# A graph attention layer: rows without neighbours in two batches, and the dense loop ahead of the last list

## The chip, the cores and the metric

One core of a Trainium2 chip. The metric is the device time of one launch in microseconds. The engines are PE (TensorE), DVE (VectorE), ACT (ScalarE), POOL (GpSimd) and SP (SyncE); each runs its own list of instructions in order and waits on semaphores.

## The reference

`x` is 8192 x 128, `adj` 8192 x 8192 int32 with about 4 ones in a row, `attn` 256 x 1.

```python
h = jnp.maximum(_layernorm(x, axis=-1), 0.0)
s_i = h @ attn[:128]
s_j = h @ attn[128:]
e = jax.nn.leaky_relu(s_i + s_j.T, negative_slope=0.2)
e = e + jnp.where(adj > 0, 0.0, -1.0e9)
out = x + jax.nn.softmax(e, axis=1) @ h
```

A row with neighbours is the softmax over those few. A row without any is a softmax over all 8192 columns, each lowered by 1e9.

## The kernel before

The 256 MB of `adj` are read once. Row `64 p + t` lies in partition `p` of tile `t`; 64 tiles make 32 pairs. `h_all`, `x_all` (64 tiles each) stay in SBUF, and `h` with its scores is also written to a table in HBM, from which rows are gathered.

For each pair `p`:

- SP loads four half tiles of 128 x 4096 int32 into the four slots of `adj_ring`. Each load waits until ACT has taken the sign of the half tile before it in its slot (`signed`).
- ACT turns a half tile into signs (bf16, L533) and counts the neighbours (`degree`). It waits for PE to have packed the half tile three before.
- PE packs the signs of eight column chunks into `words` by matmuls (`pack_tile`, L1160).
- DVE takes the largest words (`max_tile`, L656), finds the neighbours' numbers (`find_pair`, ends with `near_id`, L701), and flags rows with too many neighbours for the 12 slots of a pair (`flag_pair`). PE ranks the flagged rows (`rank_pair`, L1171), DVE gives them keys (`key_pair`), PE copies them into a list (`list_pair`).
- POOL gathers 12 neighbours for each row (`gather_pair`, L455: one indirect DMA a slot).
- Two steps later DVE scores pair `g = p - 2` (`score_pair`), ACT takes the exponential, DVE mixes (`add_pair`: 16 multiply-adds of 128 x 128, L797), SP stores the pair.

The flagged rows of eight pairs make one list of at most 128 rows with 16 slots, four lists in all (`m` 0 to 3): `find_deep` at the first step after the eight pairs, POOL's `gather_m` in parts in the steps behind it (DEEP_PARTS), `score_deep` and `add_deep` in step DEEP_MIX = 7 of the next eight, `store_m` by POOL. The last list has no next eight: its gathers and its mixing stand behind the stream. `add_deep` of list 2 stands there too, at step 31.

Rows without neighbours whose scores are extreme ("lone" rows; for all others the table's row of means serves) are handled once, behind the last pair, for at most 128 rows: `lone_mark` (which rows), `lone_compact` (one-hot matrices and ranks, PE helps, L1210 to L1213), `lone_bounds` (scores spread over the partitions by PE, L1220, L1223), then four `lone_part`s over 16 tiles of columns each: three DVE instructions of 128 x 2048 (L949, L954, L958), one exponential on ACT (L581), 16 (of 64) matmuls on PE (L1229). `lone_end` divides and adds `x`.

The dense loop ("far") is for rows that fit nowhere: it runs over `far_tiles` x `far_parts`, at least once each, and computes rows of one tile against 256 columns by the plain formula. With these inputs it runs once and stores nothing that counts. In DVE's order before: pairs 29, 30, 31 mixed, sizing of the loop (L1042 to L1069), last list (L847 to L884), `lone_end`, then the loop, which waits for POOL to have seen the last stores land (`far_free`).

Of the kernel before, what the change touches and what calls it, by code (L numbers as in the profile page):

```python
# [5 lines left out]
def graph_attention_kernel(nc: bass.Bass, x: bass.AP, adj: bass.AP, attn: bass.AP, out: bass.AP):  # L6
# [40 lines left out]
    DEEP_PARTS = (3, 3, 3, 3, 2, 2)  # L47
    DEEP_MIX = 7
# [13 lines left out]
    LC = 4  # L62
    LT = TILES // LC

# [9 lines left out]
    with ctx:  # L74
# [124 lines left out]
        lonely = end(TILES, fp32)  # L199
        lone_at, lone_top = end(TILES, fp32), end(8, fp32)  # L200
        lone_here = end(4, bf16)
        lone_key, lone_si = end(LONE, fp32), end(LONE, fp32)
        lone_eq, lone_pick = end(LONE * TILES, fp32), end(LONE * TILES, fp32)
        lone_hot = end(LONE * P, fp32).rearrange("p (k e) -> p k e", k=LONE)
        lone_few, lone_many, lone_spill = end(1, fp32), end(1, fp32), end(1, fp32)
        lost = end(TILES, fp32)
        lone_si_b, lone_max_raw, lone_max_leaky, lone_max = end(P, fp32), end(P, fp32), end(P, fp32), end(P, fp32)
        lone_absent, lone_id, lone_inv = end(1, fp32), end(1, i32), end(1, fp32)
        lone_x, lone_out = end(D, fp32), end(D, fp32)
        far_h = end(DB * COLS, fp32).rearrange("p (k c) -> p k c", k=DB)  # L210
        assert taken[0] <= HALF
        lone_p = adj_ring[:, 2:4, :].rearrange("p h w -> p (h w)").bitcast(fp32)
# [19 lines left out]
        lone_rank = words[1][:, BANK:BANK + LONE]  # L232
        lone_rec = words[1][:, BANK + 16:BANK + 17]
        lone_spread = words[0][:, BANK:BANK + P]
        lone_sum = words[2][:, BANK:BANK + ONE + 1]
# [52 lines left out]
        lone = sem("lone")  # L288
        lone_here_ready = sem("lone_here_ready")
        lone_ranked = sem("lone_ranked")  # L290
        lone_hot_ready = sem("lone_hot_ready")
        lone_spread_out = sem("lone_spread_out")
        lone_id_ready = sem("lone_id_ready")
        lone_x_in = sem("lone_x_in")
        lone_masking = sem("lone_masking")
        lone_masked = sem("lone_masked")
        lone_exp = sem("lone_exp")
        lone_summed = sem("lone_summed")
        lone_out_ready = sem("lone_out_ready")
        lone_stored = sem("lone_stored")  # L300
# [6 lines left out]
        far_h_in = sem("far_h_in")  # L307
        far_used = sem("far_used")
# [25 lines left out]
        LONE_MARK = 4  # L334
        LONE_HOT = 8
        LONE_IDS = 5
# [8 lines left out]
        def _(sp):  # L345
# [23 lines left out]
            for g in range(PAIRS - 4, PAIRS):  # L369
                store_pair(g)  # L370
# [4 lines left out]
            with sp.Fori(0, tiles) as t:  # L375
                with sp.Fori(0, parts) as c:
# [5 lines left out]
                        .then_inc(far_adj_in, 16)  # L382

        @block.gpsimd
        def _(pool):
# [63 lines left out]

            def gather_pair(p):  # L450
# [32 lines left out]

            for p in range(PAIRS):
# [9 lines left out]
            pool.indirect_dma_start(  # L494
                out=lone_x, out_offset=None, in_=x,
                in_offset=bass.IndirectOffsetOnAxis(ap=lone_id[:, 0:1], axis=0),
                bounds_check=last_row, oob_is_err=False).then_inc(lone_x_in, 16)
# [3 lines left out]
            pool.indirect_dma_start(  # L501
                out=out, out_offset=bass.IndirectOffsetOnAxis(ap=lone_id[:, 0:1], axis=0),
                in_=lone_out, in_offset=None,
# [782 lines left out]
```

## Time and profile before

| | |
|---|---|
| median of 3 runs | 868.03 us (866.7 to 868.43) |
| the profiled execution | 867.93 us |
| its span, first to last instruction | 866.2 us |
| busy share: DVE, POOL, ACT, PE | 66%, 66%, 60%, 53% |
| moved by DMA | 301.56 MB |

Times in the rows below are microseconds from the span's start. "L656" is a line of the kernel. A row of the timeline has start, duration, engine, line, operation, what it writes and reads, how many in a row, and in brackets how long its engine was idle before it and what ended that.

### The profile page before, as it was taken

How to read it: one execution, taken by the hardware profiler on the slowest of the kernel's cores; microseconds unless marked ns; L12 is line 12 of the kernel's file. 1: busy time of each engine (PE TensorE's matmuls, PEld its weight loads, DVE VectorE, ACT ScalarE, POOL GpSimd, SP SyncE). 2: the span in 40 equal slices, each digit the busy share in tenths (PEclk: the TensorE clock that was granted, in tenths of full speed). 3: DMA queues.
4: the chain of work that ended last, by engine and by line, in shares of the span. 5: the costliest groups of instructions: out<-in, count | busy, mean ns of one | idle time of the engine just before them, and what ended most of it. 6: DMA issues, size and time to landing. Idle time of an engine off the chain costs nothing.

```text
span 866.2 us, 7055 instructions
## 1 busy us (share of the span) xinstructions
PE 460.1 (53%) x1605; PEld 191.2 (22%) x1633; DVE 569.3 (66%) x2273; ACT 521.1 (60%) x357; POOL 571.0 (66%) x527
## 2 busy tenths in 40 slices
PE   0665465655555665566555656556566455623601
PEld 0332122221212222122222222222222122213600
DVE  7998266565676666656766465568656566668981
ACT  1895676666676666676666666667666677600200
POOL 6631776666567777666678777667776867758810
PEclk9998777676886678776788686876767788665955
DMA  8799999999999999999999999999999999511000
GB/s 346 286 382 404 399 406 409 410 410 410 406 408 409 410 408 409 405 410 411 404 406 410 408 411 406 414 405 412 404 405 403 408 391 404 196 25 27 18 16 14
DMA packets 39515, 301.56 MB, mean 348 GB/s; under 512 B 10611, under 2 KB 16948, under 8 KB 22065
## 3 DMA queue, kind: packets, MB, share of 16 engines
q1 hardware_dynamic: 24176, 277.23, 79.1%
q0 software_dynamic: 15296, 23.88, 8.0%
q8 instruction: 13, 0.21, 0.1%
q14 instruction: 30, 0.24, 0.1%
HBM read 303.63 MB, written 8.91 MB: 361 GB/s over the span
## 4 chain that ended last, share of the span: by engine, by line
DMA 69%; issue 13%; DVE 11%; ACT 5%; PE 1%; DVEq 0%; POOL 0%; SPq 0%; ACTq 0%; POOLq 0%
DMA adj_ring<-in_adj_dram 68%; ACT sign_ring L533 3%; DVE mixed L797 1%; DVE one_hot L609 1%; ACT h_all L544 1%; DVE adj_ring L954 1%; DVE adj_ring L958 1%; DVE adj_ring L949 1%; DVE mixed_m L879 1%; DMA x_all<-in_x_dram 1%; PE words L1160 0%; DVE codes L616 0%; DVE codes L619 0%; PE words L1220 0%; PE words L1223 0%
## 5 line engine op out<-in xcount | busy, mean ns | idle before, releaser
L533 ACT ACTIVATE sign_ring<-adj_ring,half_neg 128x4096 bf16<-128x4096 int32 x128 | 474.6, 3708 | 226.4 <-DMA adj_ring<-in_adj_dram 226.4
L455 POOL DMA_INDIRECT near<-h_table,near_id x384 | 443.8, 1156 | 198.9 <-issue 109.2
L1160 PE MATMUL words<-sign_ring,pack_w 128*128 128x512 bf16 x1004 | 357.2, 516 | 282.3 <-ACT sign_ring L533 279.6
L656 DVE MAX8 cand<-words 128x8 f32<-128x256 f32 x256 | 91.1, 418 | 223.9 <-PE words L1160 223.8
L1160 PEld LDWEIGHTS words<-sign_ring,pack_w 128*128 128x128 bf16 x1024 | 114.1, 121 | 516.7 <-ACT sign_ring L533 357.2
L797 DVE SCALAR_TENSOR_TENSOR mixed<-near,weight_n,mixed 128x128 f32<-128x128 f32 x448 | 120.3, 345 | 0.0
L470 POOL DMA_INDIRECT near_m<-h_table,id_m x64 | 79.1, 1235 | 19.5 <-issue 19.5
L1152 PE MATMUL words<-place,place_w 128*128 128x512 bf16 x120 | 47.2, 478 | 1.1 <-issue 1.0
L1142 PE MATMUL listing<-h_all 128*1 128x128 f32 x128 | 20.4, 335 | 33.7 <-ACT h_all L544 33.7
L581 ACT ACTIVATE adj_ring<-adj_ring 128x2048 f32<-128x2048 f32 x4 | 7.6, 1910 | 49.8 <-DVE adj_ring L958 49.8
L1179 PEld LDWEIGHTS listing<-cand,one_hot 128*128 128x128 f32 x128 | 28.1, 271 | 12.6 <-issue 6.5
L1229 PE MATMUL words<-h_all,adj_ring 128*128 128x129 f32 x128 | 18.8, 316 | 15.7 <-ACT adj_ring L581 15.7
L1179 PE MATMUL listing<-cand,one_hot 128*128 128x34 f32 x128 | 23.3, 317 | 2.5 <-DVE one_hot L745 2.5
L533 ACT ACTIVATION_READ_ACCUMULATOR sign_ring<-adj_ring,half_neg 128x1 f32 x128 | 23.9, 186 | 0.0
L434 POOL TENSOR_SCALAR h_all<-x_all,codes 128x128 f32<-128x128 f32 x16 | 13.0, 825 | 14.5 <-DVE codes L628 14.5
L1142 PEld LDWEIGHTS listing<-h_all 128*1 128x1 f32 x128 | 12.8, 102 | 41.4 <-issue 27.1
L672 DVE TENSOR_TENSOR codes<-cand_i,code_mask 128x512 int32<-128x512 int32 x32 | 21.9, 684 | 0.0
L1229 PEld LDWEIGHTS words<-h_all,adj_ring 128*128 128x128 f32 x128 | 18.1, 229 | 16.4 <-ACT adj_ring L581 16.4
L642 DVE TENSOR_TENSOR near<-h_all,mixed 128x2048 f32<-128x2048 f32 x8 | 21.5, 2683 | 0.0
L797 DVE SCALAR_TENSOR_TENSOR mixed<-near,weight_n,x_all 128x128 f32<-128x128 f32 x64 | 19.8, 350 | 1.1
L544 ACT ACTIVATE h_all<-x_all,codes 128x128 f32<-128x128 f32 x48 | 18.8, 480 | 0.2 <-DVE codes L628 0.2
L647 DVE TENSOR_REDUCE h_all<-near 128x16 f32<-128x2048 f32 x8 | 18.3, 2288 | 0.3
(213 smaller groups left out, 431.4 us busy)
## 6 DMA issues: line engine op xcount, KB each, us to landing
adj_ring<-in_adj_dram SPq DMA_DIRECT2D x128, 2048.0 KB, 18.9
near<-h_table,near_id POOLq DMA_INDIRECT x384, 6.4
h_table<-h_all POOLq DMA_DIRECT2D x4, 1056.0 KB, 12.2
x_all<-in_x_dram SPq DMA_DIRECT2D x4, 1024.0 KB, 9.6
out_dram<-mixed SPq DMA_DIRECT2D x32, 128.0 KB, 18.5
near_m<-h_table,id_m POOLq DMA_INDIRECT x64, 6.2
adj_ring<-h_table SPq DMA_DIRECT2D x1, 132.0 KB, 3.1
mixed<-in_L_gnn_attn_dram SPq DMA_DIRECT2D x1, 128.0 KB, 6.5
```

The costliest lines, as they stand in the source:

```text
L455: pool.indirect_dma_start(out=near[:, p % RING, k, :], out_offset=None, in_=table, in_offset=bass.IndirectOffsetOnAxis(ap=near_id[:, p % I ...
L470: pool.indirect_dma_start(out=near_m[:, k, :], out_offset=None, in_=table, in_offset=bass.IndirectOffsetOnAxis(ap=id_m[:, k:k + 1], axis=0 ...
L533: nc.scalar.activation(sign_ring[:, n % 4, :], adj_ring[:, n % 4, :], ACT.Sign, bias=half_neg[:, :], accum_out=degree[:, t, h:h + 1]).then ...
L544: nc.scalar.activation(h_all[:, t, 0:D], x_all[:, t, :], ACT.Relu, bias=shift[:, t:t + 1], scale=rstd[:, t:t + 1]).then_inc(h_ready, 1)
L656: last = nc.vector.max(out=cand[:, p % 2, t % 2, 8 * q:8 * q + 8], in_=words[t % 3][:, q * PART:(q + 1) * PART])
L672: nc.vector.tensor_tensor(codes[:, :, :, :].rearrange("p a w c -> p (a w) c"), cand_i[:, :, :].rearrange("p a w -> p (a w)").unsqueeze(2). ...
L797: ins = nc.vector.scalar_tensor_tensor(acc, near[:, e, slot, 0:D], weight_n[:, a * own + k:a * own + k + 1], base, ALU.mult, ALU.add)
L1142: last = nc.tensor.matmul(listing[0:1, 0:D], h_all[:, t, ONE:ONE + 1], h_all[:, t, 0:D], start=(t == 0), stop=(t == TILES - 1))
L1152: nc.tensor.matmul(at[:, k * BANK:(k + 1) * BANK], place_w[:, :], place[:, k * BANK:(k + 1) * BANK], start=True, stop=False)
L1160: last = nc.tensor.matmul(at[:, k * BANK:(k + 1) * BANK], pack_w[:, c, :], sign_ring[:, n % 4, o + k * BANK:o + (k + 1) * BANK], start=Fal ...
L1179: last = nc.tensor.matmul(listing[:, 0:REC], one_hot[:, p % 2, a, :], cand[:, p % 2, a, :], start=(p % SEG == 0 and a == 0), stop=(p % SEG ...
L1229: last = nc.tensor.matmul(lone_sum, lone_p[:, t * P:(t + 1) * P], h_all[:, t, 0:ONE + 1], start=(t == 0), stop=(t == TILES - 1))
```

## The change

Two batches of lone rows: batch 0 holds those of pairs 0 to 22 (at most 64 rows, four parts of 16 tiles, one of three buffers each) and is worked off in the loop, steps 22 to 30; batch 1 those of pairs 23 to 31 (at most 32 rows, two parts of 32 tiles) behind the stream. A part has 1024 elements per partition in both. Batch 0's scratch lies in the first 40 tiles of `x_all`, which are no longer read then; so the dense loop loads its tile of `x` anew (`far_x`). The dense loop stands ahead of the last list's mixing on DVE, ACT and POOL; its sizing moves up between the compaction and the bounds of batch 1, and behind its parts. The lists' gathers are made in five parts instead of six, and their mixing in step 6 instead of 7. Pair 29 is scored before tile 62's maxima and mixed before tile 63's. The stores of pairs 30 and 31 are issued by ACT.

```diff
-    DEEP_PARTS = (3, 3, 3, 3, 2, 2)
-    DEEP_MIX = 7
+    DEEP_PARTS = (3, 3, 3, 3, 4)
+    DEEP_MIX = 6
-    LC = 4
-    LT = TILES // LC
+    EARLY = 23
+    FIRST_STEP = EARLY + 1
+    LAST = 1
+    LONE_CAP = (64, 32)
+    LONE_PARTS = (4, 2)
+    LONE_BUFS = 3
+    DEAD = 40
...
@@ gpsimd
+            pool.sem_inc(far_free, 1)
...
             for p in range(PAIRS):
                 gather_pair(p)
+                if p == FIRST_STEP + 2:
+                    load_lone(0)
...
             store_m(SEGS - 2)
-            pool.wait_ge(lone_id_ready, 1)
-            pool.indirect_dma_start(out=lone_x, ...)
+            store_lone(0)
+            load_lone(LAST)
             gather_m(SEGS - 1, range(0, DEEP))
-            store_m(SEGS - 1)
-            pool.wait_ge(lone_out_ready, 1)
-            pool.indirect_dma_start(out=out, ..., in_=lone_out, ...)
             pool.wait_ge(sizes_ready, 2)
...
-            pool.wait_ge(stored_m, 16 * SEGS)
-            pool.wait_ge(lone_stored, 16)
-            pool.sem_inc(far_free, 1)
+            for e in range(2):
+                pool.wait_ge(stored[e], 16 * PAIRS // 2)
             with pool.Fori(0, tiles) as t:
...
+            store_m(SEGS - 1)
+            store_lone(LAST)
+            pool.wait_ge(stored_m, 16 * SEGS)
+            pool.wait_ge(lone_stored[0], 16)
+            pool.wait_ge(lone_stored[LAST], 16)
@@ scalar
             def exp_step(p):
...
+                if FIRST_STEP <= p - 1 < FIRST_STEP + LONE_PARTS[0]:
+                    exp_lone(0, p - 1 - FIRST_STEP)
             for p in range(1, PAIRS):
                 sign_tile(2 * p, (0,))
                 exp_step(p - 1)
                 sign_tile(2 * p, (1,))
-                sign_tile(2 * p + 1)
-            exp_step(PAIRS - 1)
+                sign_tile(2 * p + 1, (0,))
+                if p == PAIRS - 1:
+                    exp_step(p)
+                sign_tile(2 * p + 1, (1,))
...
             exp_pair(PAIRS - 2)
+            store_pair(PAIRS - 2)
             exp_pair(PAIRS - 1)
-            exp_m(SEGS - 1)
+            store_pair(PAIRS - 1)
...
+            exp_m(SEGS - 1)
@@ vector
+            def lone_step(p):
+                if p == FIRST_STEP - 2:
+                    lone_mark(0)
+                if p == FIRST_STEP - 1:
+                    lone_compact(0)
+                if p == FIRST_STEP:
+                    lone_bounds(0)
+                if 0 <= p - FIRST_STEP < LONE_PARTS[0]:
+                    lone_part(0, p - FIRST_STEP)
+                if 0 <= p - FIRST_STEP - 3 < LONE_PARTS[0]:
+                    lone_add(p - FIRST_STEP - 3)
+                if p == FIRST_STEP + 3 + LONE_PARTS[0] - 1:
+                    lone_end(0)
...
-                max_tile(2 * p)
+                if p < PAIRS - 1:
+                    max_tile(2 * p)
                 for g in mixes:
                     score_pair(g)
+                if p == PAIRS - 1:
+                    max_tile(2 * p)
...
                 key_pair(p - 1)
+                if p == PAIRS - 1:
+                    for g in mixes:
+                        add_pair(g)
                 max_tile(2 * p + 1)
...
                 if p == PAIRS - 1:
-                    lone_mark()
+                    lone_mark(LAST)
                     key_pair(p)
+                    lone_compact(LAST)
                     find_deep(SEGS - 1)
-                    add_deep(SEGS - 2)
-                    lone_compact()
-                    lone_bounds()
-                    for c in range(LC):
-                        lone_part(c)
-                for g in mixes:
-                    add_pair(g)
-                if m >= 0 and p % SEG == DEEP_MIX and p < PAIRS - 1:
+                    mark_severe()
+                    lone_bounds(LAST)
+                    for c in range(LONE_PARTS[LAST]):
+                        lone_part(LAST, c)
+                    size_loop()
+                    dve.sem_inc(far_used, 1)
+                if p < PAIRS - 1:
+                    for g in mixes:
+                        add_pair(g)
+                if m >= 0 and p % SEG == DEEP_MIX:
                     add_deep(m)
+                lone_step(p)
...
-            score_deep(SEGS - 1)
-            add_deep(SEGS - 1)
-            lone_end()
             dve.wait_ge(sizes_ready, 2)
...
-            dve.wait_ge(pair_mixed, PAIRS)
...
+            score_deep(SEGS - 1)
+            add_deep(SEGS - 1)
+            lone_end(LAST)
@@ tensor, in rank_pair
+                if p >= FIRST_STEP - 1:
+                    pe.wait_ge(lone[0], LONE_MARK + LONE_HOT)
+                if p >= FIRST_STEP:
+                    pe.wait_ge(lone_id_ready[0], 1)
+                    pe.wait_ge(lone[0], LONE_MARK + LONE_HOT + LONE_IDS)
+                if 0 <= p - FIRST_STEP - 3 < LONE_PARTS[0]:
+                    pe.wait_ge(lone[0], LONE_MARK + LONE_HOT + LONE_IDS + p - FIRST_STEP - 2)
```

`mark_severe` and `size_loop` are the old sizing (L1042 to L1069) cut in two. `lone_add` adds a part's PSUM sum to an accumulator in SBUF. In PE's order, `lone_ranks(0)` stands at the end of step 23, `lone_spreads(0)` of step 24, the matmuls of batch 0's parts of steps 26 to 29.

## Rows read from the trace of the kernel before

**Rows 1.** The head of the page.

```profile
span 866.2 us, 7055 instructions
```

**Rows 2.** Engines' busy time in one pair's stretch (instructions), granted clock, DMA share, GB/s.

```profile
core 0: us, PE busy (x) PEld busy (x) DVE busy (x) ACT busy (x) POOL busy (x), PEclk, DMA share, GB/s
670.00:692.00 22.00, 11.11 (x37) 3.88 (x35) 13.53 (x60) 14.97 (x8) 17.59 (x15) 0.74 1.00 401
```

**Rows 3.** Timeline: a ranking on PE, DVE's next step, ACT's last sign.

```profile
612.53 0.17 PE L1171 MATMUL rank<-flag,before 128*128 128x2 bf16 x1
...
617.34 1.42 DVE L656 MAX8 cand<-words 128x8 f32<-128x256 f32 x4
...
755.26 3.71 ACT L533 ACTIVATE sign_ring<-adj_ring,half_neg 128x4096 bf16<-128x4096 int32 x1 [1.42 <-DMA adj_ring<-in_adj_dram]
```

**Rows 4.** Timeline of DVE: maxima of tiles 61, 62, 63.

```profile
740.02 1.43 DVE L656 MAX8 cand<-words 128x8 f32<-128x256 f32 x4 [7.54 <-PE words L1160]
...
752.43 1.42 DVE L656 MAX8 cand<-words 128x8 f32<-128x256 f32 x4 [1.44 <-PE words L1160]
...
762.71 1.43 DVE L656 MAX8 cand<-words 128x8 f32<-128x256 f32 x4 [5.60 <-PE words L1160]
```

**Rows 5.** Timeline of DVE behind the stream, up to the lone rows' end.

```profile
768.71 0.16 DVE L735 TENSOR_TENSOR prior<-prior,flag 128x1 bf16<-128x1 bf16 x1
...
771.80 0.19 DVE L810 CAST cand_m<-listing 128x32 int32<-128x32 f32 x1 [1.16 <-PE listing L1179]
...
786.20 0.29 DVE L933 COPY adj_ring<-words 128x128 f32<-128x128 f32 x1 [2.92 <-PE words L1223]
...
787.33 2.28 DVE L949 TENSOR_TENSOR adj_ring<-adj_ring,h_all 128x2048 f32<-128x2048 f32 x1
...
814.81 0.16 DVE L779 TENSOR_REDUCE total<-weight 128x2 f32<-128x16 f32 x1
...
819.63 0.23 DVE L753 TENSOR_SCALAR score<-near,h_all 128x8 f32<-128x8 f32 x1
...
832.48 0.19 DVE L1042 TENSOR_SCALAR one_hot<-excess 128x64 f32<-128x64 f32 x1
...
835.01 0.23 DVE L847 TENSOR_SCALAR score_m<-near_m,si_m 128x16 f32<-128x16 f32 x1
...
836.51 0.16 DVE L864 RECIPROCAL inv_m<-total_m 128x1 f32<-128x1 f32 x1 [0.38 <-ACT weight_m L553]
...
841.44 0.16 DVE L963 RECIPROCAL adj_ring<-words 128x1 f32<-128x1 f32 x1
```

**Rows 6.** Timeline: the dense loop on DVE, and its store on POOL.

```profile
847.96 0.17 DVE L1091 TENSOR_SCALAR adj_ring<-adj_ring 128x2 f32<-128x2 f32 x1 [5.90 <-POOLq L511]
...
850.42 0.29 DVE L1101 TENSOR_SCALAR adj_ring<-adj_ring 128x256 f32<-128x256 int32 x1 [1.82 <-DMA adj_ring<-in_adj_dram]
...
858.31 0.35 DVE L1128 SCALAR_TENSOR_TENSOR adj_ring<-adj_ring,x_all 128x128 f32<-128x128 f32 x1 [0.24 <-DVE adj_ring L1126]
859.49 0.99 POOL L516 DMA_INDIRECT out_dram<-adj_ring  x1 [15.35 <-DVE adj_ring L1128]
```

**Rows 7.** Timeline of POOL behind the stream; last, list gathers from issue to landing.

```profile
767.69 1.00 POOL L455 DMA_INDIRECT near<-h_table,near_id  x1 [5.39 <-DVE near_id L701]
...
790.80 2.01 POOL L470 DMA_INDIRECT near_m<-h_table,id_m  x1 [0.30 <-issue]
...
817.48 3.12 POOL L470 DMA_INDIRECT near_m<-h_table,id_m  x1 [0.30 <-issue]
...
823.64 1.01 POOL L470 DMA_INDIRECT near_m<-h_table,id_m  x1 [0.30 <-issue]
...
DMA to landing us min/median/max: 2.2/3.5/6.2
```

**Rows 8.** Issue to landing of the dense loop's store, then the lone rows'.

```profile
DMA to landing us min/median/max: 2.1/2.1/2.1
...
DMA to landing us min/median/max: 4.4/4.4/4.4
```

More of the change, by code:

```diff
@@ L207, in graph_attention_kernel, with early @@
-        lone_si_b, lone_max_raw, lone_max_leaky, lone_max = end(P, fp32), end(P, fp32), end(P, fp32), end(P, fp32)
-        lone_absent, lone_id, lone_inv = end(1, fp32), end(1, i32), end(1, fp32)
-        lone_x, lone_out = end(D, fp32), end(D, fp32)
+        early_x = x_all[:, 0:DEAD, :].rearrange("p t d -> p (t d)")
+        early_taken = [0]
+        def early(size, dt):
+            at = early_taken[0]
+            early_taken[0] += size
+            return early_x[:, at:at + size].bitcast(dt)
@@ new lines, in graph_attention_kernel @@
+        homes = (early, end)
+        widths = [ts.stop - ts.start for ts in LONE_TILES]
+        lost = early(TILES, fp32)
+        lonely = [home(w, fp32) for home, w in zip(homes, widths)]
+        lone_at = [home(w, fp32) for home, w in zip(homes, widths)]
+        lone_top = [home(8, fp32) for home in homes]
+        lone_here = [home(4, bf16) for home in homes]
+        lone_key, lone_si = ([home(LONE, fp32) for home in homes] for _ in range(2))
+        lone_eq, lone_pick = ([home(LONE * w, fp32) for home, w in zip(homes, widths)] for _ in range(2))
@@ L210, in graph_attention_kernel @@
+        lone_x, lone_out = ([home(D, fp32) for home in homes] for _ in range(2))
+        lone_acc = early(ONE + 1, fp32)
+        far_x = end(D, fp32)
+        lone_size = [TILES // n * e for n, e in zip(LONE_PARTS, LONE_CAP)]
+        lone_p = [[early(lone_size[0], fp32) for _ in range(LONE_BUFS)],
+                  [adj_ring[:, 2, c * lone_size[1]:(c + 1) * lone_size[1]].bitcast(fp32)
+                   for c in range(LONE_PARTS[1])]]
+        assert early_taken[0] <= DEAD * D
         far_h = end(DB * COLS, fp32).rearrange("p (k c) -> p k c", k=DB)
@@ L368, in _ @@
                     store_pair(g)
-            for g in range(PAIRS - 4, PAIRS):
+            for g in range(PAIRS - 4, PAIRS - 2):
                 store_pair(g)
@@ L508, in _ @@
             parts = pool.value_load(far_parts[0:1, 0:1], min_val=1, max_val=DC)
-            pool.wait_ge(stored_m, 16 * SEGS)
-            pool.wait_ge(lone_stored, 16)
-            pool.sem_inc(far_free, 1)
+            for e in range(2):
+                pool.wait_ge(stored[e], 16 * PAIRS // 2)
             with pool.Fori(0, tiles) as t:
@@ L564, in _, with exp_lone @@
             sign_tile(1)
+            def exp_lone(b, c):
+                part = lone_p[b][c % len(lone_p[b])]
+                act.wait_ge(lone_masked[b], c + 1)
+                nc.scalar.activation(part, part, ACT.Exp).then_inc(lone_exp[b], 1)
             def exp_step(p):
@@ L1234, in _ @@
                 .then_inc(severe_counted, 1)
+            for c in range(LONE_PARTS[LAST]):
+                lone_matmuls(LAST, c)
             pe.wait_ge(sizes_ready, 2)
```

392 lines of the change are left out of this document (226 added, 166 removed).

## The prediction, made blind

> **What bounds the kernel now.** I read the profile in this order: the page's head, a table of the engines in one stretch of the main loop, then the DVE and POOL timelines from 740 us on. The span is 866.2 us [rows 1]; the profiled execution took 867.93 us, so 1.73 us lie outside the span, and the median of the runs shown is 868.03, the same within 0.1 us. Up to about 755 us the kernel streams the adjacency matrix. A pair of tiles takes 22 us, the DMA share is 1.00, and DVE is busy 13.53 of 22 us and POOL 17.59 [rows 2]. The last half tile lands at 755.26, where ACT starts its last sign [rows 3]. Until then the memory sets the pace and the engines have air; what follows, 111 us, is a chain with DVE in nearly every link. In the last steps before the end of the stream DVE still idles: 7.54 us before 740.02, 1.44 before 752.43 and 5.60 before 762.71 [rows 4]. After 768.71 it has one wait over 1.2 us (2.92) until the dense loop starts, for which it waits 5.90 us [rows 5, 6]. Twelve instructions over the rows without neighbours, 787.33 to 814.81, are the largest block. POOL gathers the last list beneath them and has long finished when DVE comes to it at 835.01 [rows 5, 7].
>
> **Part 1: the early batch.** It adds to the loop, in steps 22 to 30 of DVE: marking, compaction and bounds (estimated 1.4, 3.2 and 1.5 us, after the old ones, which this change moves), four parts of three instructions over 1024 elements and four additions. The old parts are twelve instructions of 2048 elements in 27.48 us [rows 5], 2.29 each, so 1024 elements cost about 1.17, a part 3.5. ACT gets four exponentials of 1 us, PE 64 matmuls. The cover is the idle time of 8.5 us per pair on DVE [rows 2]; the fullest step is 24, with some 5 us added. What could reach the stream is the new wait in front of PE's ranking matmuls: PE is there at 612.53 while DVE ends that step at 617.34 [rows 3], now 5 us later with the bounds and a part. Behind that wait stands the packing of the next tile, behind the packing ACT's sign, and behind the sign the load. But a sign needs only the half tile packed three before it, and halves come each 5.5 us; two are still to spare. I cost this at nothing before 755 us. POOL gets one gather (26) and keeps 16 in steps 24 to 28 (DEEP_PARTS 3, 3, 3, 3, 4); at 1.3 us each that is 21 us of 22. With DVE's parts it will fall some 5 us behind and win it back in steps 29 to 31, where it has 12 instead of 14. A gather is used two steps after it is asked for, so nobody waits.
>
> **Part 2: the last steps of the stream.** The mixing of list 2 moves from behind the stream into step 30, and pair 29 is scored before the maxima of tile 62 and mixed before those of tile 63. DVE is free at 750.99 (752.43 less 1.44). From there: mixing list 2, 4.93 (836.51 to 841.44 [rows 5]); last addition and end of batch 0, 0.95 (estimated from lone_end's 0.6 and one more of its size); scoring pair 29, 1.4 (a pair's 6.43 behind the stream, 819.63 to 832.48 by two, less 4.82 of mixing, 814.81 to 819.63, and 0.2 for ACT [rows 5]): 758.3. Now ACT has that pair's exponential in front of its last sign, so the sign starts at 758.5 instead of 755.26. PE's pack and DVE's maxima keep their distance of 7.45 (755.26 to 762.71 [rows 3, 4]), so the maxima of tile 63 start at 766.0, 3.3 later than before. DVE itself is at 758.3 + 1.4 (maxima) + 0.7 (key) + 4.8 (mixing) = 765.2, so it idles no more. Price +3.3; taken out of the tail for it 4.9 + 4.8.
>
> **Part 3: DVE behind the stream.** Flags of pair 31: 768.87 + 3.3 = 772.2. Mark and key, 2.1 (1.8 before, two memsets more). From 771.80 to 786.20 there stood list 3's search, list 2's mixing and the compaction with a wait of 2.92 [rows 5]: 14.4 - 4.93 - 2.92 = 6.55 for search and compaction; 18 columns instead of 64 take 1.2 off: 5.3. The wait goes, since the search and the sizing now stand between the compaction and the bounds. Sizing 2.5 (832.48 to 835.01), bounds 1.4, six instructions of 1.17, 7.0. Sum 790.5. Two pairs at 6.43: 803.4, where before it was 832.48.
>
> **Part 4: the dense loop in front.** It took DVE 10.7 us, 847.96 to 858.66, of which 1.82 was a wait for its adjacency [rows 6]; with the sizes known at 790.5 its loads land some 10 us before they are used: 8.9. The entry (value loads, loop registers) is not shown alone. It costs above nothing and below the 5.90 us of idle before 847.96 [rows 6], of which most was the wait for lone_stored and the table; I take 2. The loop ends at 814.3, and DVE stands before list 3 at 815. The stores of pairs 30 and 31 leave from ACT's queue. No row shows an issue on ACT; its price lies between nothing and POOL's 1.3, and ACT has only an exponential behind it that is needed 1.4 us later: nothing.
>
> **Part 5: POOL, which now ends last.** It starts pair 31's gathers at 767.69 + 3.3 = 771.0 [rows 7]. Then come 12 gathers, store of list 2, store and load of the lone batches, list 3's x and its 16 gathers: 32 instructions at 1.31 (1.01 + 0.30 [rows 7]), 41.8, to 812.8 if nothing holds them. Something does: during DVE's long two-input instructions a gather takes 2.01, one per DVE instruction of 2.29, and in a pair's mixing one takes 3.12 [rows 7]. With instructions half as long I assume that each gather misses the next gap and waits for the second, so the 7 us of parts let 3 through instead of 5.4: +3.1 (least 0, at most 3.1 + one more instruction, 4.3). Two mixings: +2.1 each, 4.2. POOL issues the last gather at 819 and it lands 3 us later (2.2 to 6.2, median 3.5 [rows 7]): 822. So DVE waits 7 us before list 3. By the Trainium skill, page "SBUF — State Buffer", section "Who interferes with whom", a DVE instruction with two SBUF inputs takes only the shared pair's read interface and contends with GpSimd work that reads SBUF, while descriptor writing is inferred to need the write interface; taken by the letter the gathers would run free, and the sum would be the first rival's. The rows speak against that for indirect gathers.
>
> **Part 6: the end.** List 3: 835.01 to 841.44, 6.4: 828.4. The store of the list starts at 828.7, that of lone batch 1 at 830.0 (its sum is ready at 829.1). The dense loop's own store fits between 820.5 and 826. From the start of the last store to the span's end it was 6.7 us (859.49 to 866.2 [rows 6]) with a landing of 2.1; a lone store right behind a list's store took 4.4 [rows 8]. So 6.7 to 9.0; I take 8.5, near the second since the order is that one. End 838.5, 27.7 less than 866.2. Time: 867.93 - 27.7 = 840.
>
> **The rivals.** *Gathers run free or in the gaps* (no holding by DVE): last landing at 815 or before, DVE's own chain decides; 815 + 6.4 + 1.6 + 8.5 = 831.5 span, **833 us**. For it: DVE's short instructions don't hold gathers; against it the 2.01 and 3.12. *POOL later still*: it enters the tail behind time (three blocks of mixing in 747 to 765 instead of one), or every gather of list 3 is held at 2.0: 16 x 0.7 = 11 us at most, half of it likely; **846 us**, up to 851. *The early batch reaches the stream*: PE's wait at the ranking matmul, in steps 23 to 30, passes on to the loads. Each such wait is 4 to 6.5 us; all eight in full would be about 36 us, 876 us, **slower than before**. It decides from 3.5 us a step (27.7 / 8); a step that loses 1 us makes 848. Against it the spare of two half tiles, 11 us. *The change does nothing*, because the path behind the stream is not DVE's: against it, an unbroken row of DVE work from 787.33 to 841.44.
>
> **How the numbers follow.** POOL's gathers last, 836 to 844: 0.58. Rival one, 830 to 836: 0.17. POOL later still, 844 to 851: 0.15. Stream hit in part, still faster: 0.05. Stream hit in full, slower: 0.03. Nothing: 0.02. The predicted time is the first case's 840; the range 831 to 850 takes in the entry's bounds (-2 to +4), the holding (-7 to +1 and the later rival) and the end (-2 to +0.5). A measurement of this kernel tells 0.2% (about 1.7 us) from no change. Faster 0.95, same 0.02, slower 0.03.
>
> **What would show it.** Right: last adjacency landing within 1 us of 755; last sign near 758.5 behind an exponential; maxima of tile 63 at 766 without more than 1 us of idle; end of the two pairs at 803; dense loop on DVE near 805 to 814, with no wait for its adjacency; a DVE wait of about 7 us before the last list's scoring (L847 now), ended by a near_m gather that lands at 822. Wrong: the stream's end later than 757; a gather cadence of 1.3 beneath the lone parts; no DVE wait before the last list; a wait over 3 us in the dense loop.

## The result, and the profile after

| | before | after |
|---|---|---|
| median | 867.37 us (866.57 to 868.43, 4 runs) | 844.7 us (842.92 to 847.55, 4 runs) |
| profiled execution | 867.93 us | 844.35 us |
| its span | 866.2 us | 842.6 us |

The ratio is 0.974, 95% interval 0.971 to 0.977. The forecast was 840 us, range 831 to 850. A second comparison on another chip gave 0.979 (0.977 to 0.982). The kernel before took 864.0 to 864.9 us in the experiments below and 867.4 here, so the variants are compared by their ratios to it, or by times within a profile. The end of the stream alone moves from one execution to the next: in the variants that leave everything in front of it as it is, the maxima of tile 63 start between 772.0 and 775.9.

The head and DVE's and DMA's busy shares in 40 slices, of the changed kernel:

```profile
span 842.6 us, 7427 instructions
...
DVE  7997376666666556558576666568696746669962
...
DMA  8799999999999999999999999999999999951120
```

The span is 23.6 us shorter, and it divides at one place. The maxima of tile 63 on DVE start at 773.36 instead of 762.71 [rows 4], 10.65 us later. What follows them takes 69.2 us instead of 103.5. So 34.3 us were won behind that point and 10.65 given back in front of it. Of the 34.3, 32.9 lie between tile 63 and the end of pair 31's mixing on DVE, which took 69.8 us (762.71 to 832.48 [rows 4, 5]) and takes 36.9 (773.36 to 810.28): the lone parts take 7.42 us instead of 27.48, and the mixing of list 2 (4.93), that of pair 29 (4.82) and a wait of 2.92 have left this stretch.

DVE's timeline of the changed kernel: tiles 60 to 63 first, then the first instruction of each lone part, the mixing of pair 30, the dense loop's entry and end, and the last list:

```profile
744.57 1.43 DVE L715 MAX8 cand<-words 128x8 f32<-128x256 f32 x4 [9.23 <-PE words L1279]
...
748.77 1.42 DVE L715 MAX8 cand<-words 128x8 f32<-128x256 f32 x4
...
766.64 1.42 DVE L715 MAX8 cand<-words 128x8 f32<-128x256 f32 x4
...
773.36 1.42 DVE L715 MAX8 cand<-words 128x8 f32<-128x256 f32 x4
...
788.79 1.22 DVE L1060 TENSOR_TENSOR adj_ring<-adj_ring,h_all 128x1024 f32<-128x1024 f32 x1
...
792.56 1.22 DVE L1060 TENSOR_TENSOR adj_ring<-adj_ring,h_all 128x1024 f32<-128x1024 f32 x1
...
800.05 3.76 DVE L889 SCALAR_TENSOR_TENSOR mixed<-near,weight_n,mixed 128x128 f32<-128x128 f32 x14
...
812.20 0.26 DVE L1205 TENSOR_SCALAR adj_ring<-adj_ring 128x2 f32<-128x2 f32 x1 [1.91 <-issue]
...
820.70 0.35 DVE L1244 SCALAR_TENSOR_TENSOR adj_ring<-adj_ring 128x128 f32<-128x128 f32 x1 [0.26 <-DVE adj_ring L1240]
...
824.14 0.23 DVE L939 TENSOR_SCALAR score_m<-near_m,si_m 128x16 f32<-128x16 f32 x1 [3.09 <-DMA near_m<-h_table,id_m]
```

Behind the stream the order is the one that the diff wrote: dense loop first (812.20 to 821.05), without a wait for its adjacency, then 3.09 us of waiting for the last list's gathers. The tile 61 row, 748.77, answers to 740.02 of before. It is late by 8.75 us already and has no idle in front of it, so the loss lies further up. PE's timeline of the changed kernel shows it: the first matmul of each of the early batch's parts 1, 2 and 3, and the ranking of pair 30.

```profile
685.15 6.29 PE L1338 MATMUL rank<-h_all,x_all 128*64 128x129 f32 x32 [14.89 <-DVE x_all L1076]
...
710.73 5.47 PE L1338 MATMUL rank<-h_all,x_all 128*64 128x129 f32 x32 [10.99 <-DVE x_all L1079]
...
735.48 5.05 PE L1338 MATMUL rank<-h_all,x_all 128*64 128x129 f32 x32 [10.98 <-DVE x_all L1079]
...
765.00 0.16 PE L1297 MATMUL rank<-flag,before 128*128 128x2 bf16 x1 [10.73 <-DVE x_all L1079]
```

L1076 and L1079 are `lone_add`. The parts' sums share one PSUM tile, so PE may not begin part `c` before DVE has taken part `c - 1` away; and DVE does that in `lone_step`, the last thing of its step, behind the mixing and a part's three long instructions. PE stands there for 11 to 15 us, and the next tile's packing stands behind it. DVE in turn waits for that packing at the start of its next step. Its timeline, with the addition between two steps:

```profile
695.48 1.43 DVE L715 MAX8 cand<-words 128x8 f32<-128x256 f32 x4 [10.47 <-PE words L1279]
...
710.31 0.28 DVE L1079 TENSOR_TENSOR x_all<-x_all,rank 64x129 f32<-64x129 f32 x1
...
720.23 1.43 DVE L715 MAX8 cand<-words 128x8 f32<-128x256 f32 x4 [9.65 <-PE words L1279]
```

So the two engines work one after the other. DVE takes 15.1 us from the maxima to the end of the addition (695.48 to 710.59), then PE takes 9.6 for the part and the packing, up to 720.23. That makes a step of 24.75 us, and the next one, to 744.57, takes 24.34, where the stream gives a pair 22 [rows 2]. ACT's timeline: the sign that waits for that packing, and the last two instructions in front of the stream's end:

```profile
742.90 3.71 ACT L579 ACTIVATE sign_ring<-adj_ring,half_neg 128x4096 bf16<-128x4096 int32 x1 [7.91 <-PE words L1279]
...
766.76 0.22 ACT L595 ACTIVATE weight<-below 128x16 f32<-128x16 f32 x1 [10.76 <-DVE below L861]
766.88 3.69 ACT L579 ACTIVATE sign_ring<-adj_ring,half_neg 128x4096 bf16<-128x4096 int32 x1
```

The sign's wait grows step by step: 2.27 at 693.81, 5.37 at 718.57, 7.91 here. ACT comes to it every 22 us with the loads (691.54, 713.20, 734.99), and PE's packing releases it only every 24 to 25, so some 3 us are lost in each step. The loads themselves are on time: SP issues the last one at 735.0, before the change at 736.4, and between 750 and 755 us the DMA share is down to 0.05. What is late is the work on what has landed.

POOL's timeline, from pair 31's gathers on:

```profile
778.33 0.99 POOL L488 DMA_INDIRECT near<-h_table,near_id  x1 [4.02 <-DVE near_id L760]
...
791.35 0.99 POOL L488 DMA_INDIRECT near<-h_table,near_id  x1 [0.30 <-issue]
792.65 1.99 POOL L488 DMA_INDIRECT near<-h_table,near_id  x1 [0.30 <-issue]
...
801.57 3.12 POOL L503 DMA_INDIRECT near_m<-h_table,id_m  x1 [0.30 <-issue]
...
821.95 1.00 POOL L503 DMA_INDIRECT near_m<-h_table,id_m  x1 [0.30 <-issue]
...
830.94 0.99 POOL L512 DMA_INDIRECT out_dram<-mixed_m,row_m  x1 [6.66 <-DVE mixed_m L976]
832.24 0.99 POOL L528 DMA_INDIRECT out_dram<-adj_ring  x1 [0.30 <-issue]
```

Of these gathers only two are held, one beneath the lone parts (792.65) and one beneath the mixing of pair 30 (801.57). Last, the instruction with which POOL ends the program (count, least/median/greatest ns, when):

```profile
L82 POOLq DRAIN  x1: 7675/7675/7675, 834.7 to 834.7; - x1
```

It takes 7.68 us. The same instruction of the kernel before took 4.00 us, and in both it ends the span.

### The profile page after: what moved, and what is told of

The parts are those of the page before. It is cut to its first block, busy times and chain, and to the rows that moved or that the text cites. A ratio compares the mean times of both kernels' runs of the same rounds, so it can differ in the third digit from the quotient of the medians.

```text
span 842.6 us, 7427 instructions
## 1 busy us (share of the span) xinstructions
PE 461.8 (55%) x1752; PEld 205.6 (24%) x1782; DVE 569.1 (68%) x2314; ACT 519.3 (62%) x359; POOL 567.2 (67%) x529
## 4 chain that ended last, share of the span: by engine, by line
DMA 61%; issue 15%; DVE 8%; POOL 6%; PE 5%; ACT 4%; POOLq 0%; DVEq 0%
DMA adj_ring<-in_adj_dram 60%; POOL near L488 3%; ACT sign_ring L579 3%; PE words L1279 2%; PE rank L1338 2%; POOL near_m L503 2%; DVE mixed L889 2%; DVE one_hot L668 1%; ACT h_all L590 1%; DVE cand L715 1%; DMA x_all<-in_x_dram 1%; DVE codes L675 0%; DVE codes L678 0%; DVE codes L731 0%; DMA out_dram<-adj_ring 0%
## 5 line engine op out<-in xcount | busy, mean ns | idle before, releaser
L488 POOL DMA_INDIRECT near<-h_table,near_id x384 | 449.6, 1171 | 201.3 <-issue 122.5
L1279 PE MATMUL words<-sign_ring,pack_w 128*128 128x512 bf16 x1003 | 343.1, 501 | 233.6 <-ACT sign_ring L579 230.8
L503 POOL DMA_INDIRECT near_m<-h_table,id_m x64 | 68.0, 1063 | 19.5 <-issue 19.5
L1271 PE MATMUL words<-place,place_w 128*128 128x512 bf16 x119 | 45.3, 463 | 1.5 <-issue 1.5
L1338 PE MATMUL rank<-h_all,x_all 128*64 128x129 f32 x128 | 21.0, 341 | 36.9 <-DVE x_all L1079 22.0
L1305 PEld LDWEIGHTS listing<-cand,one_hot 128*128 128x128 f32 x128 | 26.4, 258 | 13.0 <-issue 5.3
L1338 PEld LDWEIGHTS rank<-h_all,x_all 128*64 128x64 f32 x128 | 20.1, 181 | 37.2 <-issue 37.1
L1338 PE MATMUL words<-h_all,adj_ring 128*32 128x129 f32 x128 | 17.1, 305 | 5.7 <-ACT adj_ring L618 5.7
L1297 PE MATMUL rank<-flag,before 128*128 128x2 bf16 x32 | 5.9, 184 | 24.9 <-DVE x_all L1079 10.7
```

The lines of the kernel that those rows point to most:

```text
L488: pool.indirect_dma_start(out=near[:, p % RING, k, :], out_offset=None, in_=table, in_offset=bass.IndirectOffsetOnAxis(ap=near_id[:, p % I ...
L503: pool.indirect_dma_start(out=near_m[:, k, :], out_offset=None, in_=table, in_offset=bass.IndirectOffsetOnAxis(ap=id_m[:, k:k + 1], axis=0 ...
L1271: nc.tensor.matmul(at[:, k * BANK:(k + 1) * BANK], place_w[:, :], place[:, k * BANK:(k + 1) * BANK], start=True, stop=False)
L1279: last = nc.tensor.matmul(at[:, k * BANK:(k + 1) * BANK], pack_w[:, c, :], sign_ring[:, n % 4, o + k * BANK:o + (k + 1) * BANK], start=Fal ...
L1305: last = nc.tensor.matmul(listing[:, 0:REC], one_hot[:, p % 2, a, :], cand[:, p % 2, a, :], start=(p % SEG == 0 and a == 0), stop=(p % SEG ...
L1338: last = nc.tensor.matmul(lone_sum[b], part[:, k * e:(k + 1) * e], h_all[:, c * lt + k, 0:ONE + 1], start=(first and k == 0), stop=(final ...
```

## The experiments

The names in the expectations: `e1_add_soon` is experiment 1 and `e8_soon_lone_first` experiment 8. The letter A stands in each for the account put first, and is spelt out there; in experiment 1 it is that the wait of PE for the early additions costs the 7 us at the stream's end. Of the others, B says that DVE's own work fills that time; C, that the last sign behind the exponential does; D, that POOL's long end comes with the stores on ACT's queue; E, with something else; F, that it grows with stores issued shortly before; G, that a gather is held until the running long DVE instruction ends; H, that the end goes by the number of POOL's DMAs; I, that it comes with the early batch's own load or store.

**1. The additions sooner.** `lone_add` moves from the end of the step to behind `key_pair(p-1)`, some 10 us up DVE's list.

```diff
@@ lone_step
-                if 0 <= p - FIRST_STEP - 3 < LONE_PARTS[0]:
-                    lone_add(p - FIRST_STEP - 3)
@@ the loop over the pairs
                 key_pair(p - 1)
+                if 0 <= p - FIRST_STEP - 3 < LONE_PARTS[0]:
+                    lone_add(p - FIRST_STEP - 3)
```

> The changed kernel, with the addition of each early part moved from the end of DVE's step to right behind the key of that step. Theory A (in the changed kernel PE waits 11 to 15 us in front of the matmuls of early parts 1, 2 and 3 for the addition of the part before, since DVE makes it only at the step's end; PE's packing, ACT's signs and DVE's last steps come 7 to 9 us late by it): those waits fall below 3 us each, the maxima of tile 61 come near 741 instead of 748.8, those of tile 63 near 766 instead of 773.4, and the end moves by as much, 7 us: 837 us, ratio to the kernel before 0.965. Theory B (DVE's own added work fills the last steps, PE's waits only lie beside it): 844 +- 1.5 us.

Measured 835.02 us (833.69 to 836.45), ratio 0.967 (0.964 to 0.971), span 833.4. DVE's timeline, tiles 61 and 63 and the last list:

```profile
738.85 1.43 DVE L715 MAX8 cand<-words 128x8 f32<-128x256 f32 x4 [7.96 <-PE words L1279]
...
764.14 1.43 DVE L715 MAX8 cand<-words 128x8 f32<-128x256 f32 x4 [0.87 <-PE words L1279]
...
814.93 0.23 DVE L939 TENSOR_SCALAR score_m<-near_m,si_m 128x16 f32<-128x16 f32 x1 [3.09 <-DMA near_m<-h_table,id_m]
```

PE's waits for DVE in those steps are gone, tile 61 is at 738.85 (740.02 before the change [rows 4]), and everything behind tile 63 has moved up by the same 9.2 us. The wait was worth 9.2 us, and A holds; B is out, since DVE's work is the same. A small wait has come in its place: the 0.87 us in front of tile 63 are for a packing whose sign stands behind pair 29's exponential on ACT, which waits 5.17 us for DVE there (756.54).

**2. The last sign first.** ACT takes the last half tile's sign before pair 29's exponential.

```diff
                 sign_tile(2 * p + 1, (0,))
+                sign_tile(2 * p + 1, (1,))
                 if p == PAIRS - 1:
                     exp_step(p)
-                sign_tile(2 * p + 1, (1,))
```

> The changed kernel, with ACT's last sign in front of pair 29's exponential instead of behind it. In the changed kernel ACT stood 10.8 us before that exponential with the last sign behind it. Theory A (DVE is busy without a gap from 748.8 to the maxima of tile 63 at 773.4, so the sign's lateness costs nothing): last sign at 756 instead of 767, time unchanged, 844 +- 1.5 us. Theory C (the late last sign is what delays the end): maxima of tile 63 earlier by 3 to 10 us and the time 835 to 841 us.

Measured 843.18 us (842.51 to 845.59), ratio 0.976 (0.973 to 0.980), between the changed kernel's two (0.974 and 0.979). The maxima of tile 63 start at 773.35, to 0.01 us where they did. The row itself had said so: no idle stands in front of 773.36, so DVE was not waiting for that sign. C falls for the changed kernel; with the additions moved up the order can cost at most the 0.87 us of experiment 1.

**3. The dense loop last again**, on DVE, ACT and POOL, all else as changed.

```diff
@@ vector (gpsimd and scalar alike)
+            score_deep(SEGS - 1)
+            add_deep(SEGS - 1)
+            lone_end(LAST)
             dve.wait_ge(sizes_ready, 2)
...
-            score_deep(SEGS - 1)
-            add_deep(SEGS - 1)
-            lone_end(LAST)
```

> The changed kernel, with the dense loop behind the last list's mixing again, on DVE, ACT and POOL; the rest of the change stays. Theory A (the loop now lies where DVE would wait for the last list's gathers, which end at 824): DVE waits some 14 us for the gathers, the loop's 8.9 us and its entry of 1.9 us come behind the lone rows' end at 831, its store starts near 842.5; with POOL's drain at the program's end as short as in the kernel before (4.0 us) the time is 850.5 us, with the drain of the changed kernel (7.7 us) 854. Rival (the order of loop and list does not matter, since the loop's loads and POOL decide): 844 us.

Measured 859.02 us (853.99 to 860.82, 8 runs), ratio 0.994 (0.991 to 0.996), span 857.2. Its loop's store starts at 846.83 and is the last, where the changed kernel's last starts at 832.24. DVE waits 15.07 us for the last list's gathers. Against the ratios 0.974 and 0.979 the order is worth 12 to 17 us. In the profiles it is 12.0: the spans differ by 14.6, of which 2.6 were there at tile 63 (775.92). That is more than expected, and half or more of what the change won. In front there is cover for the loop: the gathers of the last list, which POOL must issue anyway.

**4. One part alone, on the kernel before**: the gathers in five parts and the lists mixed in step 6, so that list 2 is mixed before the stream ends.

```diff
-    DEEP_PARTS = (3, 3, 3, 3, 2, 2)
-    DEEP_MIX = 7
+    DEEP_PARTS = (3, 3, 3, 3, 4)
+    DEEP_MIX = 6
...
                     find_deep(SEGS - 1)
-                    add_deep(SEGS - 2)
```

> The kernel before, with one part of the change: the lists' gathers in five parts and their mixing in step 6 of eight, so that list 2 is mixed in step 30 instead of behind the stream. Theory A (step 30 has 8.9 us of idle time on DVE, which takes the 5.0 us of mixing): 868.0 - 5.0 = 863 us, ratio 0.994. Rival (the maxima of the last tiles come later by as much, or POOL's fuller step 28 delays them): 867.5 to 868.5, ratio 1.0.

Measured 860.26 us (856.05 to 861.71, 9 runs), ratio 0.995 (0.993 to 0.997), by which 4.2 us were won. DVE's maxima of tile 63 start at 762.02 with 5.34 us of idle in front (762.71 and 5.60 before [rows 4]): the 4.9 us of mixing found room in front of it and cost nothing there.

**5. The last pairs' stores on SP again.**

```diff
@@ sync
-            for g in range(PAIRS - 4, PAIRS - 2):
+            for g in range(PAIRS - 4, PAIRS):
                 store_pair(g)
@@ scalar
             exp_pair(PAIRS - 2)
-            store_pair(PAIRS - 2)
             exp_pair(PAIRS - 1)
-            store_pair(PAIRS - 1)
```

> The changed kernel, with the stores of pairs 30 and 31 issued by SP again instead of ACT. In every kernel with the change POOL's drain at the end of the program took 7.7 us, in those without it 3.8 to 4.0. Theory D (ACT's DMA queue, used nowhere else, lengthens the drain): drain 4.0 us, time 3.7 us less than the changed kernel's, ratio about 0.970. Theory E (the drain hangs on something else in the change): drain 7.7 us, ratio 0.974. In both the issue on ACT itself is worth nothing, so DVE's times stay within 0.5 us.

Measured 848.42 us (846.68 to 850.14), ratio 0.982 (0.978 to 0.986). POOL's last instruction takes 7.68 us as before, so D falls. But the expectation of unchanged DVE times was wrong. DVE's timeline at the loop's entry:

```profile
817.97 0.17 DVE L1203 TENSOR_SCALAR adj_ring<-adj_ring 128x2 f32<-128x2 f32 x1 [5.27 <-DMA adj_ring<-h_table]
...
821.66 0.36 DVE L1213 TENSOR_SCALAR adj_ring<-adj_ring 128x256 f32<-128x256 int32 x1 [3.05 <-DMA adj_ring<-in_adj_dram]
```

SP's loads for the loop stand behind the two stores, which wait for the pairs to be mixed: the first leaves at 815.11 instead of 799.25, and DVE waits 5.27 and 3.05 us where the changed kernel waits 1.91 and nothing. The loop's last instruction on DVE comes at 829.55 instead of 820.70. Of that 8.85 us, 2.5 were there at tile 63 in this execution (775.89), and 3.1 are taken from the wait for the gathers, which is gone; the last store starts 5.8 us later. So in the profiles moving two stores to ACT's queue was worth some 3 us, because of what stood behind them on SP's; the ratios, 0.982 against 0.974 and 0.979, agree in direction and are too wide apart to give a size.

**6. Without the store of lone batch 1.**

```diff
             store_m(SEGS - 1)
-            store_lone(LAST)
+            pool.wait_ge(lone_out_ready[LAST], 1)
             pool.wait_ge(stored_m, 16 * SEGS)
             pool.wait_ge(lone_stored[0], 16)
-            pool.wait_ge(lone_stored[LAST], 16)
```

> The changed kernel without the store of lone batch 1 (its rows keep what the pairs' stores wrote). Theory F (the drain grows with the indirect stores that POOL has issued shortly before): last store is the list's at 830.9 and the drain falls to about 4 us: 837.5 to 839 us. Theory E: the drain stays 7.7 us and only the 1.3 us of the store itself is saved: 843 us.

Measured 845.52 us (2 runs), ratio 0.979 (0.975 to 0.983). POOL's last instruction takes 7.59 us, though the store that stood last before it is gone. F falls.

**7. Batch 1 in one part**: three DVE instructions of 2048 elements for six of 1024.

```diff
-    LONE_PARTS = (4, 2)
+    LONE_PARTS = (4, 1)
```

> The changed kernel with batch 1's two parts of 1024 elements joined to one of 2048: DVE does the same elements in three instructions instead of six. Theory G (a gather on POOL is held up to the end of the DVE instruction it falls into, so instructions of 2.3 us hold each gather 1 us while those of 1.2 us mostly don't): the gathers beneath the part take 2.0 us each, three or four of them, POOL's last gather comes 2 to 3 us later and the end with it: 846 to 847 us. Rival (the length of the instruction does not matter, only the elements): the same gathers take 1.0 us with at most one of 2.0 and the time is 844 +- 1 us.

Measured 847.98 us (2 runs, 845.94 and 850.02), ratio 0.982 (0.978 to 0.987). POOL's timeline beneath the three instructions (788.33, 790.65 and 793.05 on DVE, 2.29 each):

```profile
789.60 1.89 POOL L488 DMA_INDIRECT near<-h_table,near_id  x1 [0.30 <-issue]
791.79 2.02 POOL L488 DMA_INDIRECT near<-h_table,near_id  x1 [0.30 <-issue]
794.12 2.09 POOL L488 DMA_INDIRECT near<-h_table,near_id  x1 [0.31 <-issue]
```

All three are held, where beneath the same elements in six instructions of 1.22 us one was. Pair 31's first gather to the last list's last now takes 45.7 us (777.89 to 823.57) instead of 43.6. Each of the three ends 0.87 us after the DVE instruction that was running when it started: 791.49, 793.81 and 796.21 against 790.62, 792.94 and 795.34. So a gather is held to the end of that instruction, and G holds. The changed kernel shows the same in its two cases: 792.65 starts just inside the instruction from 792.56 to 793.78 and ends at 794.64, and 801.57 ends at 804.69, 0.88 us after the unbroken row of pair 30's mixing (803.81). The gathers at 788.75, 790.05 and 791.35 went free although DVE was as busy. They started just where a DVE instruction started (788.79, 790.04, 791.42), since the two rhythms, 1.30 and some 1.25 us, are nearly equal. How much of the small holding is owed to that no run shows, and neither is why other gathers pass within a row of mixing.

**8. Experiment 1, and lone batch 1 ended and stored before the last list**, in the 3 us in which DVE waits for the list's gathers.

```diff
-            store_m(SEGS - 1)
             store_lone(LAST)
+            store_m(SEGS - 1)
...
+            lone_end(LAST)
             score_deep(SEGS - 1)
             add_deep(SEGS - 1)
-            lone_end(LAST)
```

> The kernel with the early additions moved up (e1_add_soon), and also the end of lone batch 1 in front of the last list's scoring on DVE, where DVE waits 3.1 us for the gathers, and its store in front of the list's store on POOL. Theory A (the end is a chain: last gather's landing, list mixing, two stores one behind the other, drain): the lone store leaves the chain, 1.3 us less than e1_add_soon in the span, 832.1; POOL's last store starts at 821.7. Rival (DVE's half microsecond for the lone rows now lies in front of the list instead of behind it and nothing is won): 833.4.

Measured 832.32 us (831.12 to 834.58), ratio 0.963 (0.960 to 0.965), span 830.1. The lone store starts at 815.47, the list's is last, at 819.81. From DVE's start on the last list to the last store it is 6.84 us instead of experiment 1's 8.09, so 1.25 us are won there, as expected. The rest of the 3.3 us between the two spans is chance: tile 63 was 3.2 us sooner in this execution (760.93), and one more gather was held behind it (2.06 us at 796.60).

**9. Experiment 8, and the stores of list 2 and lone batch 0 in front of pair 31's gathers**, where POOL idled 4.02 us.

```diff
             for p in range(PAIRS):
+                if p == PAIRS - 1:
+                    store_m(SEGS - 2)
+                    store_lone(0)
                 gather_pair(p)
...
-            store_m(SEGS - 2)
-            store_lone(0)
             load_lone(LAST)
```

> e8_soon_lone_first, and also the stores of list 2 and of lone batch 0 in front of pair 31's gathers, where POOL idles 5 us. Theory A (with the early additions moved up, POOL's row of 32 instructions ends last and DVE waits 3.1 us for it): POOL's last gather starts 2.6 us earlier, DVE's wait falls to about 0.5 us, span 829.5. Rival (POOL's gathers were held by DVE's instructions anyway, in other places): less than 1 us.

Measured 831.59 us (827.29 to 833.49), ratio 0.961 (0.957 to 0.965), span 828.9. The last gather starts at 809.37, the last store at 818.60. DVE has no wait for the gathers left; its own chain ends last. From tile 63 (763.34) to the span's end it is 65.6 us, against 69.2 in experiment 8, where one gather more was held for some 1.2 us. The rest, some 2.4 us, is what the two stores took from the row of gathers; 2.6 were expected. By the intervals of the whole time it can't be told from experiment 8, but both beat the kernel before and the changed one clearly.

**10. The changed kernel without the load of `x` and the store of lone batch 0.**

```diff
-                if p == FIRST_STEP + 2:
-                    load_lone(0)
...
-            store_lone(0)
             load_lone(LAST)
```

> The changed kernel without the load of x and without the store of lone batch 0 (its rows keep what the pairs' stores wrote). It has as many DMAs from POOL as the kernel before. Theory H (POOL's drain at the end depends on how many DMAs POOL has issued in all): drain 3.8 to 4.0 us, span about 836 us. Theory E (it depends on something else in the change): drain 7.7 us, and only the 1.3 us of the store itself is saved in the row of gathers: span about 841 us.

One run, 838.11 us, span 836.4, against 846.45 for the changed kernel on the same chip (experiment 11). The program's end on POOL:

```profile
L82 POOLq DRAIN  x1: 3837/3837/3837, 832.3 to 832.3; - x1
```

That is what H forecast. Letter I would give the same, since this kernel changes both the number of DMAs and the early batch's own; experiment 12 parts the two.

**11. The changed kernel on the same chip as 8, 9 and 10.**

> The changed kernel as it is, on the chip of these runs, so that the variants are compared with it and not only with the kernel before. All theories: ratio to the kernel before 0.974 +- 0.004.

Measured 846.45 us (842.98 to 849.3), ratio 0.979 (0.977 to 0.982). Its last instruction on POOL takes 7.68 us.

**12. The kernel before with two more indirect DMAs**: the lone rows' `x` gathered three times, which makes 466 DMAs issued by POOL, as in the changed kernel.

```diff
             pool.wait_ge(lone_id_ready, 1)
-            pool.indirect_dma_start(
+            for r in range(3):
+              if r > 0:
+                pool.wait_ge(lone_x_in, 16 * r)
+              pool.indirect_dma_start(
                 out=lone_x, out_offset=None, in_=x,
...
-                dve.wait_ge(lone_x_in, 16)
+                dve.wait_ge(lone_x_in, 48)
```

> The kernel before, with the gather of the lone rows' x made three times instead of once, one after the other. POOL issues two DMAs more, as many as the changed kernel; the last list's gathers end at about 831 instead of 825, still ahead of DVE, which comes for them at 835. Theory H (POOL's drain at the program's end depends on the number of DMAs that POOL has issued): drain 7.7 us instead of 4.0, span 870, ratio 1.004. Theory I (it depends on the changed kernel's own early load and store, which this kernel has not): drain 3.8 to 4.0 us, ratio 1.000.

Measured 864.22 us (10 runs), ratio 1.001 (0.999 to 1.003).

```profile
L74 POOLq DRAIN  x1: 4161/4161/4161, 860.4 to 860.4; - x1
```

H falls. The nine kernels with the early batch's load and store end with 7.6 to 7.7 us on POOL, the four without (before, 4, 10, 12) with 3.8 to 4.2. I is what is left; which of the two DMAs does it, and how, is open and wasn't tried.

## Why the prediction was right, and where it was off

**The direction and the size.** Forecast 27.7 us less span, measured 23.6. The mechanism was right: DVE's work behind the stream was the path, it shrank as forecast, and POOL's row of gathers then ended last. Three terms were off: the stream's end and the program's end cost more, the holding of gathers less. That the sum came within 4.1 us is in part luck, since errors of 9.3 us one way met 5.2 the other.

**Part 1, the early batch: the step that failed.** "I cost this at nothing before 755 us" held for the loads (735.0 against 736.4) and not for the packing. The step listed 64 matmuls for PE and looked at one wait, in front of the ranking. It did not ask whom part `c`'s matmuls wait for. The kernel says it: one `lone_sum` for all parts, and a `lone_add` at the end of DVE's step. The spare of two half tiles, 11 us, takes up a wait that comes once; here PE waits for DVE and DVE for PE in each of these steps, 24 to 25 us round instead of 22, and the lateness grows: 2.27, 5.37, 7.91 on ACT. The idle time of 8.5 us per pair was no cover for it, because DVE's idle time was now spent waiting for PE. Experiment 1 prices it at 9.2 us. A slip beside it costs nothing: POOL had 14 gathers in steps 28 and 29 of the kernel before, and 12 in 30 and 31, not 14 up to 31, and it idles before pair 31's gathers anyway (4.02 us).

**Part 2, the last steps.** The price of 3.3 became 10.65, 7.3 us more, and all of it from part 1. Without it, in experiment 1, tile 63 is at 764.14, +1.4: the estimate itself was then 1.9 us too high (its own terms, DVE ready at 765.2 and the maxima at 766.0, left 0.8 us of idle where it says none), and experiment 4 shows the mixing of list 2 to be free. That the last sign stands behind an exponential was priced as part of the +3.3; experiment 2 shows it to cost nothing while DVE is late, and experiment 1 at most 0.87 us when it isn't.

**Part 3, DVE behind the stream.** Right: 17.7 us from the flags (779.52) to the sizes (797.23), forecast 18.3; the two pairs end at 810.3, forecast 803.4 plus the 7.3 that came in.

**Part 4, the loop in front.** Right: 8.85 us against 8.9, entry 1.91 against 2, no wait for the adjacency. One sign was badly chosen: "a wait over 3 us in the dense loop" was to speak against the forecast. DVE does wait 3.58 us there for PE's matmuls (before 819.78), but it waited 3.56 for them in the kernel before too (before 857.40), inside the 10.7 us from which the 8.9 were taken. That its loads find SP's queue free is owed to the stores on ACT, which were counted at nothing as a cost (0.34 to 0.39 us each, right) and were in truth a gain of 3 us (experiment 5).

**Part 5, POOL ends last.** The mechanism was right: DVE waits for a near_m gather. The size of the holding was not. Forecast 7.3 us over lone parts and mixings (on 41.8 for the row itself, where 32 times 1.31 is 41.9); measured, the row on POOL from pair 31's first gather to the list's last lasts 43.6 us instead of 48 and some 3.1 of it is holding. "Each gather misses the next gap and waits for the second" is wrong: a held gather waits for the end of the one instruction running, or of the row of multiply-adds (experiment 7). Beneath instructions of 1.22 us one gather takes 1.99, the others 1.00; beneath one mixing one takes 3.12, beneath the other none. So the last gather starts at 821.95 instead of 819, in spite of 7.3 us of lateness, and DVE's wait is 3.09 instead of 7. The Trainium skill, page "SBUF — State Buffer", section "Who interferes with whom", was read to the effect that two-input DVE instructions leave descriptor writing alone; the rows of before [rows 7] and experiment 7 speak against that for indirect gathers: all three beneath long instructions are held by 0.9 to 1.1 us.

**Part 6, the end.** From the last store's start to the span's end I took 8.5, bounds 6.7 to 9.0; it was 10.36, outside. The stores land in 2.2 us each, less than the 4.4 assumed for the second, and the last one's start to the start of POOL's last instruction is 2.5 us in both kernels (859.49 to 862.0, 832.24 to 834.7). The term overlooked was that last instruction itself, 7.68 instead of 4.00 us.

**The sum.** The stream's end +7.3; the row on POOL -4.4; from its last issue to DVE's start -0.8; from there to the last store +0.1; the end +1.9: together +4.1, from 838.5 to 842.6. The rival "gathers run free" had the small holding, "POOL later still" the late entry. Neither held as put. Of the third, "the early batch reaches the stream", the wait came at another instruction and cost a fourth of its full price, 9.2 of some 36 us.

## What to carry to other kernels

For every wait that a diff adds, look where the signal is given, not only where it is awaited: a cheap addition at the end of one engine's step can hold another engine's whole queue. If that engine's result starts the first one's next step, the two no longer overlap; add up the round trip and compare it with the pace of the stream. Spare buffers only put the loss off, and it grows with each step. Put such a release at the first place where its inputs are ready.

An independent loop is well placed where an engine would otherwise wait for the gathers of the next stage. Its loads leave early only if nothing that waits stands before them in the same queue.

## What the runs showed of the hardware

- POOL's instruction at the program's end took 3.8 to 4.2 us in four kernels and 7.6 to 7.7 in nine. It was long where the early batch's load and store were issued. Neither the number of POOL's DMAs (464 with 3.84 and 4.00 us, 466 with 4.16 and 7.68, 465 with 7.59) nor the last store decides it.
- An indirect gather is issued in 1.00 us and 0.30 between two. It took 1.89 to 2.09 beneath DVE instructions of 2.29 us, mostly 1.00 beneath ones of 1.22 us, and 2.06 to 3.12 once in some rows of 16 short multiply-adds and not at all in others. Held gathers ended 0.87 us after the DVE instruction of 2.29 us that was running when they started (experiment 7), and 0.88 us after a whole row of multiply-adds (the changed kernel, 801.57).
